# A quantised attention stage: weights prepared on GpSimd ahead of the stage, the first sequence quantised ahead, and two of a step's operations in another order

## What is computed

```python
def _div_clamp_fp8(x, scale):
    y = jnp.clip(x.astype(jnp.float32) / scale, -448.0, 448.0)
    y = y.astype(jnp.bfloat16).astype(jnp.float32)
    return _fp8_roundtrip(y)              # float8_e4m3fn and back

def _fp8_linear_pertensor(x, wq, w_scale, in_scale):
    xq = _div_clamp_fp8(x, in_scale)
    return jnp.einsum('bsi,oi->bso', xq * in_scale, wq) * w_scale
```

## Time and profile before

| | us |
|---|---|
| median of 3 runs | 2275.6 |
| lowest and highest of them | 2272.78, 2278.18 |
| the profiled execution's own time | 2279.39 |
| its span, first to last instruction | 2277.6 |

### The profile page before, as it was taken

How to read it: one execution, slowest core, us unless ns; L and a number is a source line. 1 busy time by engine, 2 the same in 40 slices (tenths; PEclk the granted TensorE clock), 3 DMA queues, 4 the chain that set the end, 5 groups by cost and what they waited for, 6 DMA issues and landing times.

```text
span 2277.6 us, 32744 instructions
## 1 busy us (share of the span) xinstructions
PE 1897.8 (83%) x11446; PEld 1395.2 (61%) x11446; DVE 1494.5 (66%) x2588; ACT 1111.4 (49%) x2532; POOL 1027.5 (45%) x734
## 2 busy tenths in 40 slices
PE   7677788787999875699999999768888789977999
PEld 6111166544899663577777777657777665544888
DVE  5698933475654573566666666569999958756443
ACT  4444422253232346666565665556766536633443
POOL 2699921121910331344454444479999920012231
PEclk9688888698999996899999999989999989998999
DMA  4111001201100301000000000100000020000000
GB/s 153 42 33 33 0 1 72 111 0 56 56 0 0 149 5 55 1 1 1 1 1 1 1 1 22 34 1 1 1 1 1 26 76 1 1 0 1 6 8 8
DMA packets 22164, 54.82 MB, mean 24 GB/s; under 512 B 8463, under 2 KB 13752, under 8 KB 19592
## 3 DMA queue, kind: packets, MB, share of 16 engines
q1 hardware_dynamic: 22024, 53.01, 7.0%
HBM read 44.61 MB, written 1.05 MB: 20 GB/s over the span
## 4 chain that ended last, share of the span: by engine, by line
PE 45%; DVE 22%; issue 12%; ACT 11%; POOL 9%; SPq 1%; DMA 0%; DVEq 0%; POOLq 0%; ACTq 0%
POOL sbuf L1270 4%; DVE sbuf L2255 3%; PE psum L4096 3%; DVE sbuf L2925 3%; PE psum L4157 2%; POOL sbuf L1278 2%; PE psum L3475 2%; ACT sbuf L1844 2%; PE psum L4144 2%; DVE psum L3060 1%; PE psum L4583 1%; PE psum L4604 1%; PE psum L4590 1%; DVE sbuf L2917 1%; PE psum L4100 1%
## 5 line engine op out<-in xcount | busy, mean ns | idle before, releaser
L1270 POOL TENSOR_TENSOR sbuf<-sbuf 128x1035 f32<-128x1035 f32 x128 | 248.4, 1971 | 0.9 <-ACT sbuf L1912 0.9
L4230 PE MATMUL psum<-sbuf 128*128 128x128 f32 (+1 forms) x1024 | 143.3, 290 | 58.7 <-ACT sbuf L1921 43.0
L1921 ACT ACTIVATE sbuf<-sbuf 128x1001 f32<-128x1001 f32 (+1 forms) x128 | 141.6, 1139 | 100.8 <-DVE sbuf L3068 65.0
L4230 PEld LDWEIGHTS psum<-sbuf 128*128 128x128 f32 (+1 forms) x1024 | 125.6, 152 | 79.8 <-ACT sbuf L1921 58.1
L1232 POOL TENSOR_TENSOR sbuf<-sbuf 128x512 f32<-128x512 f32 x64 | 69.6, 1087 | 217.2 <-DVE sbuf L2942 217.2
L1111 POOL TENSOR_TENSOR sbuf<-sbuf 128x1024 f32<-128x1024 f32 x64 | 149.9, 2354 | 16.1 <-DVE sbuf L2255 15.2
L2255 DVE TENSOR_TENSOR_SCAN sbuf<-psum,sbuf 128x1024 f32<-128x1024 f32 x64 | 144.5, 2278 | 14.0 <-POOL sbuf L1111 7.7
L3423 PE MATMUL psum<-sbuf 96*128 96x512 bf16 x256 | 83.9, 439 | 74.3 <-DVE sbuf L2255 33.1
L4096 PE MATMUL psum<-sbuf 128*128 128x512 f32 x256 | 124.3, 609 | 17.4 <-DVE sbuf L2904 17.4
L3060 DVE SCALAR_TENSOR_TENSOR psum<-sbuf,psum 128x1024 f32<-128x1024 f32 (+1 forms) x96 | 122.3, 1274 | 14.2 <-PE psum L4220 7.0
L1391 ACT ACTIVATE psum<-psum,sbuf 128x1016 f32<-128x1016 f32 x64 | 68.9, 1081 | 125.5 <-PE psum L3423 125.5
(11 more groups left out here) (899 smaller groups left out, 5153.6 us busy)
## 6 DMA issues: line engine op xcount, KB each, us to landing
sbuf<-sbuf SPq DMA_DIRECT2D x42, 128.0 KB, 2.4
sbuf<-w_p_d SPq DMA_DIRECT2D x8, 512.0 KB, 3.6
sbuf<-w_qkv_d SPq DMA_DIRECT2D x3, 768.0 KB, 4.3
sbuf<-w_e_d SPq DMA_DIRECT2D x1, 2048.0 KB, 7.7
sbuf<-w_gu_d SPq DMA_DIRECT2D x1, 2048.0 KB, 9.4
sbuf<-w_gu_d SPq DMA_DIRECT2D x2, 1024.0 KB, 7.9
sbuf<-w_dn_d SPq DMA_DIRECT2D x1, 2048.0 KB, 16.4
sbuf<-w_q_d SPq DMA_DIRECT2D x1, 2048.0 KB, 8.3
```

The lines of the kernel that those rows point to most:

```text
L1270: pool.tensor_tensor(P_r[g % 7][:, :, :], rows.unsqueeze(2).to_broadcast([128, 23, 45]), cols.unsqueeze(1).to_broadcast([128, 23, 45]), AL ...
L1921: act.activation(Q_r[g % 6][:, 0:w], Q_r[g % 6][:, 0:w], ACT.Silu, scale=q8_p[n % 2][:, h:h + 1]).then_inc(silu_done, 1)
L4230: last = pe.matmul(Gps[0:m, c, :], Q_r[g % 6][:, 128 * c:128 * c + m], ident[:, :], start=h == 0 and c % 4 == 0, stop=h == 7, skip_group_c ...
```

## The change

Six things change, all of them around L2x.

1. **Weights.** The scaling and centring leave ACT and DVE for POOL. There they stand where `L2x_split` stood, ahead of L2a: 8 scalings, and for each of 8 blocks a tree of seven additions, one multiplication by -1/128 and one addition (L1179 to L1218 of the new file). For this `w_q2`, `w_qx2` and `w_kv2` change places in SBUF with the bf16 parts `w_p3`, and their three loads are issued when L1x has ended instead of at the end of L1f. Keys' and values' weights are loaded before L1a. PE waits once for all of it.
2. **The split of the projection's weights** moves from L1f into L2a and the first eight rounds of L2x. Its first two copies go to ACT (`L2x_hi`, `L2x_mid`), the two subtractions stay on POOL (`L2x_rest`, `L2x_lo`, the latter writing bf16 itself).
3. **Sequence 0** is normalised, transposed and half quantised inside L2a, and the other half right behind the last residual.
4. **ACT** makes the probabilities' copy ahead of the roots.
5. **DVE** quantises (and takes the statistics) ahead of the reciprocal.
6. POOL clears `keys` in round 8 of L2x instead of before it, and the loads of L2f are issued behind the projection's weights.

The core of the diff:

```diff
+            def L2x_scale(j, w, factor):
+                pool.tensor_tensor(w, w, factor.unsqueeze(2).to_broadcast([128, w.shape[1], 128]), ALU.mult).then_inc(scaled_done, 1)
+            def L2x_centre(j, w, heads):
+                pool.tensor_tensor(wtree[:, 0:heads, 0:64], w[:, :, 0:64], w[:, :, 64:128], ALU.add).then_inc(sums_done, 1)
+                for s in range(6):
+                    half = 32 >> s
+                    pool.wait_ge(sums_done, L2x_start['sums'] + 8 * j + s + 1)
+                    pool.tensor_tensor(wtree[:, 0:heads, 0:half], wtree[:, 0:heads, 0:half], wtree[:, 0:heads, half:2 * half], ALU.add).then_inc(sums_done, 1)
...
+                pool.tensor_tensor(w, w, wmean[:, 0:heads].unsqueeze(2).to_broadcast([128, heads, 128]), ALU.add).then_inc(centred_done, 1)
...
+            def L2x_rest(q):
+                part = slice(4 * q, 4 * q + 4)
                 pool.wait_ge(hi_done, L2x_start['hi'] + q + 1)
                 pool.tensor_tensor(p_raw[q % 2][:, :, :], p_raw[q % 2][:, :, :], w_p3[0][:, part, :], ALU.subtract).then_inc(rest_done, 1)
...
+            def L2x_lo(q):
+                part = slice(4 * q, 4 * q + 4)
                 pool.wait_ge(mid_done, L2x_start['mid'] + q + 1)
+                pool.tensor_tensor(w_p3[2][:, part, :], p_raw[q % 2][:, :, :], w_p3[1][:, part, :], ALU.subtract).then_inc(lo_done, 1)
...
@@ POOL, L2a
                 L2a_sub(i, 0)
                 L2a_sub(i, 1)
+                if i % 2 == 0:
+                    L2x_rest(i // 2)
+                else:
+                    L2x_lo(i // 2)
@@ POOL, L2x
+                if i < 8:
+                    if i % 2 == 0:
+                        L2x_rest(4 + i // 2)
+                    else:
+                        L2x_lo(4 + i // 2)
@@ ACT, L2a, at the end of round i
+                if i % 2 == 0:
+                    if i == 0:
+                        act.wait_ge(L1f_matmul_done, 138)
+                    L2x_hi(i // 2)
+                else:
+                    L2x_mid(i // 2)
+                if i == 5:
+                    L2x_factor(0)
+                if i == 7:
+                    act.wait_ge(L2x_w_loaded, 96)
+                    L2x_unT(0)
@@ ACT, L2x
-            L2x_factor(0)
-            L2x_scale_weights(0)
-            L2x_unT(0)
-            L2x_scale_weights(1)
             for i in range(66):
...
                     L2x_vc(i)
-                    L2x_rstd(i)
                 if i >= 2:
                     L2x_pTc(i - 2)
+                if i < 64:
+                    L2x_rstd(i)
                 if 1 <= i < 65:
                     L2x_exp(i - 1)
-                if i < 6:
-                    L2x_scale_weights(i + 2)
+                if i % 2 == 1 and i < 8:
+                    L2x_mid(4 + i // 2)
+                    if i < 7:
+                        L2x_hi(5 + i // 2)
@@ DVE, L2a
+                if i == 7:
+                    L2x_u(0)
                 if i > 0:
                     L2a_scale(i - 1)
                     L2a_resid(i - 1)
+                if i == 7:
+                    L2x_quantise(0)
+                    L2x_quantise(1)
...
+                if i == 8:
+                    L2x_quantise(2)
+                    L2x_quantise(3)
@@ DVE, L2x
                     L2x_max(i - 1)
-                    L2x_recip(i - 1)
-                if i < 6:
-                    L2x_centre_weights(i + 2)
...
                     if s in (3, 4, 5, 6):
                         L2x_quantise(4 * n + s - 3)
+                if 1 <= i < 65:
+                    L2x_recip(i - 1)
@@ PE
+                if i == 7:
+                    L2x_uTr(0)
...
-                if n == 0:
-                    pe.wait_ge(centred_done, L2x_start['centred'] + i + 1)
+                if i == 0:
+                    pe.wait_ge(centred_done, L2x_start['centred'] + 8)
...
-                if i == 0:
-                    pe.wait_ge(lo_done, L2x_start['lo'] + 8)
+                if i < 8:
+                    pe.wait_ge(lo_done, L2x_start['lo'] + i + 1)
```

More of the change, by code:

```diff
@@ L481, in build_program @@
         L2a_table = view(sbuf, 9472, [2, 8, 128])
-        L2a_P = [view(sbuf, 46152 + 1024 * a, [8, 128]) for a in range(2)]
+        L2a_P = [view(sbuf, 3328 + 1024 * a, [8, 128]) for a in range(2)]
         L2a_PT = [view(sbuf, 48200 + 1024 * a, [8, 128]) for a in range(2)]
@@ L991, in _ @@
             sp.dma_start(smo[:, :], smo_d).then_inc(L2x_w_loaded, 16)
[L992 removed]
+            for q in range(2, 8):
+                sp.wait_ge(lo_done, L2x_start['lo'] + q - 1)
+                sp.dma_start(p_raw[q % 2][:, :, :], w_p2_d[:, 4 * q:4 * q + 4, :]).then_inc((L2x_p0_loaded, L2x_p1_loaded)[q % 2], 16)
             sp.wait_ge(L2a_w_loaded, 32)
@@ new lines, in L2x_heads @@
+            def L2x_heads(w):
+                return w.rearrange('p (h d) -> p h d', d=128)
+            pool.wait_ge(L2x_c_loaded, 64)
+            pool.tensor_tensor(wfs[:, :, :], insc[:, :, :], wsc[:, 0:4].unsqueeze(2).to_broadcast([128, 4, 2]), ALU.mult).then_inc(const_done, 1)
+            pool.wait_ge(const_done, L2x_start['const'] + 1)
+            for c in range(2):
+                L2x_scale(c, L2x_heads(w_v2[:, c, :]), wfs[:, 3, c:c + 1])
+            for c in range(2):
+                L2x_scale(2 + c, L2x_heads(w_k2[:, c, :]), wfs[:, 2, c:c + 1])
@@ new lines, in _ @@
+            for c in range(2):
+                pool.wait_ge(scaled_done, L2x_start['scaled'] + 3 + c)
+                L2x_centre(c, L2x_heads(w_k2[:, c, :]), 8)
+            pool.wait_ge(L2x_w_loaded, 96)
+            for c in range(2):
+                L2x_scale(4 + c, L2x_heads(w_q2[:, c, :]), wfs[:, 0, c:c + 1])
+            for c in range(2):
+                pool.wait_ge(scaled_done, L2x_start['scaled'] + 5 + c)
+                L2x_centre(2 + c, L2x_heads(w_q2[:, c, :]), 16)
+            for c in range(2):
+                L2x_scale(6 + c, L2x_heads(w_qx2[:, c, :]), wfs[:, 1, c:c + 1])
@@ L1184, in L2x_split @@
+            for c in range(2):
+                pool.wait_ge(scaled_done, L2x_start['scaled'] + 7 + c)
+                L2x_centre(4 + c, L2x_heads(w_qx2[:, c, :]), 16)
+            for c in range(2):
+                L2x_centre(6 + c, L2x_heads(w_kv2[:, c, 0:1024]), 8)
+            def L2x_rest(q):
                 part = slice(4 * q, 4 * q + 4)
-                pool.wait_ge((L2x_p0_loaded, L2x_p1_loaded)[q % 2], 16 * (q // 2) + 16)
-                pool.tensor_copy(w_p3[0][:, part, :], p_raw[q % 2][:, :, :]).then_inc(hi_done, 1)
@@ L1193, in L2x_split @@
-                pool.wait_ge(rest_done, 2 * q + 2)
-                pool.tensor_copy(w_p3[2][:, part, :], p_raw[q % 2][:, :, :]).then_inc(lo_done, 1)
-            pool.wait_ge(resid_done, L1x_start['resid'] + 8)
-            for q in range(8):
-                L2x_split(q)
+                pool.tensor_tensor(w_p3[2][:, part, :], p_raw[q % 2][:, :, :], w_p3[1][:, part, :], ALU.subtract).then_inc(lo_done, 1)
             def L2a_norm(n):
@@ L1714, in _, with L2x_factor, L2x_unT, L2x_hi @@
                 act.activation(unT1[:, 0:2, :], ps1[:, 0, 0:256], ACT.Copy).then_inc(L1f_scalar_done, 1)
+            def L2x_factor(n):
+                act.wait_ge(stats_done, L2x_start['stats'] + n + 1)
+                act.activation(st0[:, 8:9], st0[:, 7:8], ACT.Ln, scale=1.0 + 1e-5, bias=eps2[:, 0:1]).then_inc(ln_done, 1)
+                act.wait_ge(ln_done, L2x_start['ln'] + n + 1)
+                act.activation(st0[:, 9:10], st0[:, 8:9], ACT.Exp, scale=-0.5).then_inc(factor_done, 1)
+            def L2x_unT(n):
+                act.wait_ge(uT_done, L2x_start['uT'] + n + 1)
+                if n > 0:
+                    act.wait_ge(ratio_done, L2x_start['ratio'] + 4 * n)
+                for c in range(2):
+                    last = act.activation(unT0[:, c, :], (L2x_uT_first if n == 0 else L2x_uT)[:, c, :], ACT.Identity, scale=lnb2[:, 0, c:c + 1], bias=lnb2[:, 1, c:c + 1])
+                last.then_inc(unT_done, 1)
+            def L2x_hi(q):
+                act.wait_ge((L2x_p0_loaded, L2x_p1_loaded)[q % 2], 16 * (q // 2) + 16)
+                act.activation(w_p3[0][:, 4 * q:4 * q + 4, :], p_raw[q % 2][:, :, :], ACT.Copy).then_inc(hi_done, 1)
+            def L2x_mid(q):
+                act.wait_ge(rest_done, q + 1)
+                act.activation(w_p3[1][:, 4 * q:4 * q + 4, :], p_raw[q % 2][:, :, :], ACT.Copy).then_inc(mid_done, 1)
             def L2a_rstd(a, b, c):
@@ L3989, in _, with L2x_uTr @@
                 last.then_inc(L1f_matmul_done, 1)
+            def L2x_uTr(n):
+                pe.wait_ge(u_done, L2x_start['u'] + n + 1)
+                out = L2x_uT_first if n == 0 else L2x_uT
+                for c in range(2):
+                    last = pe.transpose(out[:, c, :], u0[:, 128 * c:128 * c + 128], ident[:, :])
+                last.then_inc(uT_done, 1)
             def L2a_uTr(n):
```

182 lines of the change are left out of this document (61 added, 121 removed).

## The result

The changed kernel is no faster: its median is 2287.72 us (five runs, 2282.69 to 2288.97), where the kernel before takes 2275.6. The ratio is 1.0047, with a 95% interval of 1.0031 to 1.0063, so it is slower by about half a per cent. The prediction said 2204. The profiled execution has a span of 2286.0 us (before 2277.6). Ratios compare the fast runs of one session, in which the kernel before ran too, so they can differ in the last digits from the quotient of two medians printed here.

The account below looks back on a forecast made before the run. TensorE bounds L1f and, but for a 0.33 us gap, plain L2x steps; VectorE bounds quantised ones. 3 + 6 - 14.5 - 31 - 35 = -71.5 us takes 2279.39 to 2207.9, by median 2204 us; range 2190 to 2228.

Parts of the forecast that it names:

- L1f: L1f: POOL does the weights from 575 to about 665 us; its long operations hold VectorE up, +3 us.
- The slower rival: Before L2a's first normalising: POOL's weights work beyond 754 us adds one for one; 2296 us at 270 us work; chance 0.03.
- L2a: L2a's rounds: a loop through ACT's copy, POOL's subtraction and normalising takes 10.9 us instead of 9.79; +6 us.
- The hand-over: L2a's end to TensorE's first L2x product (P): P 3.9 us after the last residual's start; net 14.5 us saved.
- The first eight steps: From TensorE's first L2x product to step 7's maximum: 108.7 us falls to 78 without weights, 31 saved.
- P stays late: Start of L2x: sequence 0's quantisation falls behind the last residual, P keeps its 20 us; 2218 us; chance 0.10.
- POOL's long operations hold up L1f: First two rounds of L1f: four-microsecond POOL operations stand in the way, 17 us instead of 3; 2218 us; chance 0.10.
- The steps after M7: L2x from step 7's maximum to step 63's: 18.2 us from TensorE's gap, 17.0 from quantised steps, together 35 us saved.
- ACT's slack is too thin: L2x steps: ACT's 0.15 us slack fails, plain steps stay 8.20 us, quantised about 8.4; 2227 us; chance 0.15.
- Behind L2x: From step 63's maximum to L3f's last residual: no change predicted, 0 us.

Follow-up runs that it names:

- e1: The changed kernel, but POOL's product wfs raises and awaits load counter L2x_c_loaded instead of shared const_done; 2205.93 us, ratio 0.9681.
- e3: e1 with POOL's subtractions of the split in L2a one round later, behind the next normalising; 2201.36 us, ratio 0.9662.
- e4: e1 with ACT's roots ahead of the copy of the probabilities again; 2220.39 us, ratio 0.9753.

## Why the prediction was wrong

- **The step that failed** is the start of POOL's work, in the prediction's part on L1f: "55 to 90 us, from 575 to about 665, far ahead of 754", and with it the rival's "From 575 there are 179 us". The weights ran from 749.14 to 835.37, some 174 us late, and L2a's first normalising came 79.4 us later than before instead of on time. The amount was right (86.2 us), if by two errors that partly cancel: scalings and additions of means are 24 x 1024 columns in the trace and not 16, at 1.9 us for 1024 and not 2.13. The start was taken from the loads and from POOL's idle time; the wait L1198, which the change adds on POOL, was not followed to the one who releases it. All that was needed was on the page of code: who raises `const_done`, how often before L2x, and on which engine the ninth count stands.
- **The slower rival** had the right place and the right price, one for one, and the wrong trigger: it let the amount of work decide (250 us), where the start of the work did. With the start at 749 the point from which it decides was long passed, at 86 us. That the result, 2287.7 us, lies near its 2296 is a coincidence. Its chance of 0.03 was the chance of a threefold miscount, not that of a late start, which it did not consider.
- **L2a**, +6 and +2.5: measured +7.2 after and +9.6 in e1. With the loop opened (e3) 3.2 us stay, against the 2.5 for what stands behind the rounds, so the loop cost 4.0 us in the changed kernel and 6.4 in e1, against 6.
- **The hand-over**, -17: measured -16.9. (Its own terms, 19.95 - 3.4 - 2.5, make 14.0 us and not the 14.5 in the sum.) **The first eight steps**, -31: measured -29.4 and, in e1, -32.3; the 3 us between them lie right behind P and go with TensorE's clock there (0.67 and 0.84), for which there was no term. The rivals by which P stays late and by which POOL's long operations hold up L1f by 17 us fell.
- **The steps after M7**, -35: measured -38.1. The 31 plain steps saved 14.7 us where 10.2 were counted, since most came to 7.66 us instead of 7.87; I counted only TensorE's gap of 0.33, and did not follow where the other 0.2 went. The 24 quantised ones saved 23.4, where 25 were counted. The rival by which ACT's slack is too thin fell. (With quantised steps at 8.4, as it says, it should have lost 19 us and not 23; e4 has steps of 8.20 of both kinds.)
- **L1f**, +3: measured 0.0 with the weights there.
- **Behind L2x**, 0: measured +6.2 (+5.9 in e1), of which the next section tells.

With the hold gone the sum is -70.7 against -71.5 predicted, and e1's 2205.93 us against 2204. That this is so close is partly luck: L1f and the steps of L2x came out better by 3.0, 1.3 and 3.0 us, and L2a, the start and the stages behind L2x worse by 1.1, 0.9 and 5.9. The mechanisms of the terms held; the last of these differences has nothing to do with any of them.

## What to carry to other kernels

When a step moves to another engine, its waits move with it, and a counter that several stages raise keeps its meaning only on the engine in whose order the values were counted. For each wait that a change adds or moves, write down the event that brings the last count, the engine it is on and its time in the trace; a wait on the engine's own result that names a shared counter is the one to suspect. And a rival on the amount of work needs a twin on its start.
